# A decoder step on one core: quantising by masks on exponent bits, four scatters moved into the expert tiles, and a flag made on chip

## What is computed

```python
x = layernorm(x + tanh_attention(x))
x = layernorm(x + cross_attention(context, context, x, mask))
x = layernorm(x + quantised_linear(x))
x = layernorm(x + normed_attention(x))
x = layernorm(x + sparsemax_attention(x, context, context))
x = layernorm(x + mixture_of_experts(x))
```

```python
scales = max(max(abs(blocks), axis=-1) / 7.5, 1e-30)
q = nearest_on_grid(blocks / scales)      # 0, 0.125 ... 7.5; a tie goes to the lower value
out = (xq * xs) @ (wq * ws).T + bias
```

```python
topk_ids, topk_val = argmax(logits), max(logits)
xs = x * sigmoid(topk_val)
routed = (silu(xs @ gate[e]) * (xs @ up[e])) @ down[e]     # e = topk_ids of the row
out = shared + routed
```

## Time and profile before

| | us |
|---|---|
| median of the runs | 3414.75 |
| lowest and highest run | 3407.99, 3420.42 |
| the profiled execution, its own time | 3409.47 |
| its span in the trace | 3407.8 |
| quantised stage, 1245 to 1384 | 139 |
| sparsemax stage, 1795 to 2984 | 1189 |
| small stage of the flag, up to the first load of the expert stage | 2989 to 2994 |
| route block, 2994 to 3164 | 170 |
| expert tiles, 3164 to 3408 | 244 |

### The profile page before, as it was taken

One profiled execution on the slowest core, in us unless ns is written; L12 is line 12 of the kernel. 1 busy time (PEld: TensorE's weight loads), 2 busy tenths in 40 slices (PEclk: granted clock), 3 DMA queues, 4 the chain that ended last, 5 costly groups with the idle time before them and its releaser, 6 DMA issues. The chain is left out here.

```text
span 3407.8 us, 70871 instructions
## 1 busy us (share of the span) xinstructions
PE 2892.1 (85%) x23440; PEld 1868.3 (55%) x23440; DVE 2300.0 (67%) x10040; ACT 1990.0 (58%) x5876; POOL 1525.7 (45%) x2396
## 2 busy tenths in 40 slices
PE   8999997799999943599985888888888888779897
PEld 4555565476766732355552444454445444456897
DVE  2444545477777779467665999999999999622232
ACT  3333331477777730377763989898889988731111
POOL 0122212356666536566652444445454444405454
PEclk9999998799999976799986889888998988789999
DMA  2000000211111101100101000000000000063796
GB/s 75 14 23 15 18 13 17 61 46 44 47 44 47 43 27 46 42 27 27 31 23 44 17 23 20 23 18 19 23 20 23 20 23 16 5 234 145 266 350 221
DMA packets 106071, 190.86 MB, mean 56 GB/s; under 512 B 11891, under 2 KB 86906, under 8 KB 100446
## 3 DMA queue, kind: packets, MB, share of 16 engines
q1 hardware_dynamic: 101374, 176.34, 15.6%
q0 software_dynamic: 4320, 9.86, 0.8%
HBM read 145.22 MB, written 42.90 MB: 55 GB/s over the span
## 5 line engine op out<-in xcount | busy, mean ns | idle before, releaser
L3099 DVE MAX8 sa_cand<-sa_s 128x8 f32<-128x45 f32 (+3 forms) x3328 | 399.7, 190 | 31.2 <-ACT sa_s L2945 31.2
L914 ACT ACTIVATE ca_p<-ca_sm,ca_nb 100x361 f32<-100x361 f32 x512 | 301.0, 589 | 173.7 <-DVE ca_nb L995 173.3
L729 POOL TENSOR_SCALAR ca_p<-ca_p,ca_rec 100x361 f32<-100x361 f32 x512 | 282.2, 573 | 250.0 <-DVE ca_rec L1009 250.0
L2704 POOL TENSOR_SCALAR sa_s<-sa_s,sa_unit,sa_nu 128x361 f32<-128x361 f32 (+1 forms) x416 | 261.8, 651 | 204.0 <-DVE sa_nu L3191 204.0
L523 DVE RECIPROCAL ta_rec<-ta_den 128x400 f32<-128x400 f32 x64 | 169.6, 2650 | 246.4 <-PE ta_den L384 246.4
L2828 PE MATMUL sa_tr<-sa_ident,sa_s 128*128 128x128 f32 (+3 forms) x1248 | 230.1, 304 | 113.0 <-ACT sa_pT L2979 98.5
L995 DVE CUSTOM_DVE_ANT_0 ca_sm<-ca_sc,ca_mb 100x361 f32<-100x361 f32 x512 | 249.8, 526 | 59.5 <-PE ca_sc L816 59.4
L2961 ACT ACTIVATE sa_spare_a<-sa_s,sa_nu 128x361 bf16<-128x361 f32 (+1 forms) x416 | 247.3, 595 | 57.4 <-DVE sa_nu L3193 57.4
L2694 POOL TENSOR_TENSOR sa_over<-sa_cand,sa_tc 128x280 f32<-128x280 f32 (+3 forms) x128 | 99.6, 778 | 400.5 <-DVE sa_tc L3118 262.9
L288 POOL TENSOR_SCALAR_AFFINE_SELECT ta_pT<-ta_pT 100x400 f32<-100x400 f32 x128 | 66.6, 545 | 450.7 <-ACT ta_pT L466 450.7
L2828 PEld LDWEIGHTS sa_tr<-sa_ident,sa_s 128*128 128x128 f32 (+3 forms) x1248 | 164.8, 160 | 181.9 <-ACT sa_pT L2979 127.5
(11 more groups left out here) (314 smaller groups left out, 7195.1 us busy)
## 6 DMA issues: line engine op xcount, KB each, us to landing
me_we<-m_experts SPq DMA_DIRECT2D x40, 1024.0 KB, 7.1
me_wd<-m_experts SPq DMA_DIRECT2D x40, 512.0 KB
ca_cTs<-cT SPq DMA_DIRECT2D x32, 361.0 KB
sa_cTs<-cT SPq DMA_DIRECT2D x32, 361.0 KB
rows_acc<-me_zeros SPq DMA_DIRECT2D x1, 7196.0 KB
rows_in<-me_zeros SPq DMA_DIRECT2D x1, 7168.0 KB
ea_near<-rows_acc SPq DMA_DIRECT2D x40, 128.5 KB, 5.6
ea_xe<-rows_in SPq DMA_DIRECT2D x40, 128.0 KB
```

The costliest lines, as they stand in the source:

```text
L729: ins = pool.tensor_scalar(p[:, r, j, :], p[:, r, j, :], rec[:, r, j:j + 1], 1.0, ALU.mult, ALU.mult)
L914: act.activation(p[:, r, j, :], sm[:, r % 2, j, :], ACT.Exp, bias=nb[:, r % 2, j:j + 1], scale=-1.0, accum_out=den[:, r, j:j + 1]).then_in ...
L2704: pool.tensor_scalar(s[0:rows, u, i, :], s[0:rows, u, i, :], unit[0:rows, :], nu2[0:rows, i:i + 1], ALU.mult, ALU.add).then_inc(p_done.sem, 1)
L3099: ins = dve.max(cand[0:rows, i, q, :], s[0:rows, u, i, PART[q]:PART[q + 1]])
```

## The change

**In the quantised stage** the scale that divides is kept apart from half of it, which multiplies the result. The power of two of each number is now taken from its bits: one mask keeps the exponent (`pw`), another keeps and inverts it (`fl`), so that a product with the second brings the number near one; there it is rounded in one instruction by a constant, ties are put right in two, and one more multiplies by the power. The chain has 12 instructions.

**Between the sparsemax and the expert stage** PE transposes `top` into one row, and DVE makes the flag of it in the same block; the store of `sum_max`, the wait for it, and the stage `unfinished` are gone.

**In the expert stage** the couples 10 and 11 (tiles 20 to 23), the last in `DOWNS`, aren't scattered in the route block but by POOL at the start of `expert_tiles`. SP loads the rows of the first four tiles in the route block, once all scatters to `rows_in` have landed, and one identity serves both blocks.

```diff
-                chain.then(dve.tensor_scalar(scale_, amax[:, 0:nb], 1 / 7.5, 1e-30, ALU.mult, ALU.max))
-                chain.then(dve.reciprocal(inv[:, 0:nb], scale_))
+                chain.then(dve.tensor_scalar(amax[:, 0:nb], amax[:, 0:nb], 1 / 7.5, 1e-30, ALU.mult, ALU.max))
+                dve.tensor_scalar(scale_, amax[:, 0:nb], 0.5, None, ALU.mult)
+                chain.then(dve.reciprocal(inv[:, 0:nb], amax[:, 0:nb]))
...
-                chain.then(dve.tensor_tensor(near_, t, t, ALU.mult))
-                dve.tensor_scalar(tied, near_, 4.0, ONE, ALU.is_ge, ALU.mult)
-                chain.then(dve.tensor_scalar(magic, near_, 16.0, 2 * ONE, ALU.is_ge, ALU.mult))
-                chain.then(dve.scalar_tensor_tensor(magic, tied, ONE, magic, ALU.add, ALU.add))
-                chain.then(dve.tensor_tensor(near_, t, magic, ALU.add))
-                chain.then(dve.tensor_tensor(near_, near_, magic, ALU.subtract))
-                chain.then(dve.tensor_tensor(tied, near_, t, ALU.subtract))
-                chain.then(dve.scalar_tensor_tensor(tied, tied, 2 * PER, magic, ALU.mult, ALU.is_ge))
-                chain.then(dve.scalar_tensor_tensor(tied, tied, 1 / PER, magic, ALU.mult, ALU.mult))
-                dve.tensor_tensor(near_, near_, tied, ALU.subtract).then_inc(done, 1)
+                dve.tensor_scalar(bits(power), bits(t), EXPONENT, None, ALU.bitwise_and)
+                chain.then(dve.tensor_scalar(bits(flip), bits(t), EXPONENT, EXPONENT, ALU.bitwise_and, ALU.bitwise_xor))
+                chain.then(dve.scalar_tensor_tensor(t, flip, 2.0, t, ALU.min, ALU.mult))
+                chain.then(dve.tensor_scalar(near_, t, MAGIC, MAGIC, ALU.add, ALU.subtract))
+                chain.then(dve.scalar_tensor_tensor(t, near_, STEP / 2, t, ALU.subtract, ALU.is_equal))
+                chain.then(dve.scalar_tensor_tensor(near_, t, -STEP, near_, ALU.mult, ALU.add))
+                dve.scalar_tensor_tensor(near_, power, 1.0, near_, ALU.max, ALU.mult).then_inc(done, 1)
...
-            sp.wait_ge(top_step, 1)
-            sp.dma_start(sum_max, top[:, :]).then_inc(top_out, 16)
             for u in range(2):
                 sp.wait_ge(*stored[u].at(B // 2, 0))
-            sp.wait_ge(top_out, 16)
...
+            pe.wait_ge(top_step, 1)
+            pe.transpose(proj[0:1, 0:S], top[:, :], ident[0:S, 0:S]).then_inc(top_turned, 1)
...
+            dve.wait_ge(top_turned, 1)
+            dve.tensor_reduce(high[:, :], proj[0:1, 0:S], AX.X, ALU.max).then_inc(top_step, 1)
+            dve.wait_ge(top_step, 2)
+            dve.tensor_scalar(late[:, :], high[:, :], 1.0 + SUM_ERROR, None, ALU.is_gt).then_inc(top_step, 1)
+            dve.wait_ge(top_step, 3)
+            dve.tensor_copy(flag, late[:, :]).then_inc(top_step, 1)
+            dve.wait_ge(top_step, 4)
...
-            sp.wait_ge(early_in, 2 * DEEP * 16)
+            sp.wait_ge(rows_sent, 1)
+            rows_in_t = rows_in.rearrange("(t p) d -> t p d", p=P)
+            for n in range(DEEP):
+                sp.dma_start(xe[:, n, :], rows_in_t[n]).then_inc(early_in, 16)
+            sp.wait_ge(early_in, 3 * DEEP * 16)
...
+                    if n not in late_tiles():
+                        pool.indirect_dma_start(rows_acc, bass.IndirectOffsetOnAxis(ap=slot_i[:, n:n + 1], axis=0),
+                                                acc[:, n, :], None).then_inc(acc_sent, 16)
+                if d == COUPLES - 4:
+                    pool.wait_ge(sent, 16 * TILES)
+                    pool.sem_inc(rows_sent, 1)
...
+                if i or not loaded:
+                    sp.wait_ge(*etr_done.at(n, 1 - DEEP))
+                    sp.dma_start(xe[:, s, :], rows_in_t[first + n]).then_inc(xe_in[s].sem, 16)
...
-            identity(pool, ident, setup, 0)
             pool.memset(half[:, :], -0.5).then_inc(setup, 1)
-            pool.wait_ge(setup, 3)
+            if loaded:
+                for n in late_tiles():
+                    pool.indirect_dma_start(rows_acc, bass.IndirectOffsetOnAxis(ap=slot_i[:, n:n + 1], axis=0),
+                                            acc[:, n, :], None).then_inc(acc_sent, 16)
+            pool.wait_ge(setup, 1)
```

More of the change, by code:

```diff
@@ L1071, in quantised_linear @@
     NB = X_COLS // BLOCK
-    ONE = 1.5 * 2.0 ** 20
-    PER = 1.5 * 2.0 ** 23
-    STEPS = 13
+    EXPONENT = 0x7F800000
+    STEP = 0.25
+    MAGIC = STEP * 1.5 * 2.0 ** 23
+    STEPS = 10
     with ExitStack() as ctx:
@@ L2428, in _, with packed_sparse_attention @@
             dve.tensor_reduce(top[:, :], worst[:, :], AX.X, ALU.max).then_inc(top_step, 1)
-def packed_sparse_attention(nc, x, cT, heads4, Wq, bq, Wk, bk, Wv, bv, WoS, bo, out, sum_max):
+def packed_sparse_attention(nc, x, cT, heads4, Wq, bq, Wk, bk, Wv, bv, WoS, bo, out, flag):
     H, HD = 16, 16
@@ L2497, in packed_sparse_attention @@
         top = a.sb("top", [S, 1])
+        high = a.sb("high", [1, 1])
+        late = a.sb("late", [1, 1])
         pT = a.sb("pT", [P, NK, H * S])
@@ L3738, in _, with late_tiles, expert_tiles @@
                 add_shared(d)
-def expert_tiles(nc, tag, experts, rows_in, rows_acc, out, owner_i, first, count, we, wd, loaded, acc_sent):
+def late_tiles():
+    couples = (TILES + 1) // 2
+    last = couples - 3
+    return [n for c in range(last, couples - 1) for n in range(2 * c, 2 * c + 2)]
+def expert_tiles(nc, tag, experts, rows_in, rows_acc, acc, slot_i, out, owner_i, first, count, we, wd, xe, ident, loaded, acc_sent):
     with ExitStack() as ctx:
         a = Place(nc, ctx, tag)
-        ident = a.sb("ident", [P, P])
-        xe = a.sb("xe", [P, DEEP, D])
         xeT = a.sb("xeT", [P, 2, D])
@@ L3839, in _ @@
             open_all(pe, etr_done, g_done, up_done, y_done)
-            pe.wait_ge(setup, 2)
             def turn_rows(n):
                 s = n % DEEP
-                pe.wait_ge(*xe_in[s].at(n // DEEP, 1))
+                pe.wait_ge(*xe_in[s].at(n // DEEP, 0 if loaded else 1))
                 pe.wait_ge(*eT_done.at(n, -1))
@@ L3948 @@
 SUM_ERROR = 2.0 ** -17
-def unfinished(nc, sum_max, flag):
-    with ExitStack() as ctx:
-        a = Place(nc, ctx, "uf")
-        row = a.sb("row", [1, S])
-        high = a.sb("high", [1, 1])
-        late = a.sb("late", [1, 1])
-        row_in = a.sem("row_in")
-        step = a.sem("step")
-        block = ctx.enter_context(nc.Block())
-        @block.sync
-        def _(sp):
-            sp.dma_start(row[:, :], sum_max.rearrange("s o -> o s")).then_inc(row_in, 16)
-        @block.vector
-        def _(dve):
-            dve.wait_ge(row_in, 16)
-            dve.tensor_reduce(high[:, :], row[:, :], AX.X, ALU.max).then_inc(step, 1)
-            dve.wait_ge(step, 1)
-            dve.tensor_scalar(late[:, :], high[:, :], 1.0 + SUM_ERROR, None, ALU.is_gt).then_inc(step, 1)
-            dve.wait_ge(step, 2)
-            dve.tensor_copy(flag, late[:, :]).then_inc(step, 1)
-            dve.wait_ge(step, 3)
 def build(nc, t):
@@ L3986, in build @@
     normed_attention(nc, rows[2], t["parity01"], t["causal"], t["a1_WkqT"], t["a1_WvT"], t["a1_WuT"], t["a1_ln"], rows[3])
-    sums = [dram(f"sum_max{n}", (S, 1)) for n in range(2)]
+    sum_max = dram("sum_max", (S, 1))
     sparse = lambda newton, tag, sum_max: sparse_attention(
@@ L3990, in build @@
         t["c1_Wo"], t["c1_bo"], rows[4], sum_max, newton, tag)
-    packed_sparse_attention(nc, rows[3], t["cT"], t["heads4"], t["c1_Wq"], t["c1_bq"], t["c1_Wk"], t["c1_bk"], t["c1_Wv"],
-                            t["c1_bv"], t["c1_WoS"], t["c1_bo"], rows[4], sums[0])
     with nc.sbuf_tensor("late", [1, 1], I32) as flag:
-        unfinished(nc, sums[0], flag[:, :])
+        packed_sparse_attention(nc, rows[3], t["cT"], t["heads4"], t["c1_Wq"], t["c1_bq"], t["c1_Wk"], t["c1_bk"], t["c1_Wv"],
+                                t["c1_bv"], t["c1_WoS"], t["c1_bo"], rows[4], flag[:, :])
         late = nc.values_load(flag[0:1, 0:1], min_val=0, max_val=1)
         with nc.If(late == 1):
-            sparse(ALL_STEPS, "sb", sums[1])
+            sparse(ALL_STEPS, "sb", sum_max)
         mixture_of_experts(nc, rows[4], t["m_gate"], t["m_shared"], t["m_experts"], t["m_consts"],
```

26 lines of the change are left out of this document (12 added, 14 removed).

## The result

The changed kernel takes 3380.13 us in the median (3378.05 to 3382.45), the one before beside it 3414.15: 34.0 us less, a ratio of 0.990 with a 95% interval of 0.988 to 0.991. The prediction was 3375, with a range from 3361 to 3389.

What follows compares the result with a forecast made beforehand. It took three limits: a DVE instruction chain, a hand-over in which nothing computes, and a wait for a tiny transfer. −27.3 − 8.3 − 4.1 = −39.7 us from the 3414.75 median gave 3375, range 3361 to 3389.

Steps and rivals of the forecast that it cites:

- Part 1: Quantised stage: a shorter DVE chain gives −28.1 us, less 0.8 for a late load: −27.3, ends −24 and −28.
- The price of the masks on int32: Quantised stage: each int32 mask over 1280 columns takes 0.82 us; at 1.49, 8.0 us less gain, chance 0.08.
- the load: Quantised stage: SP's load of the group three ahead, behind the normed rows' store, lands 0.4 us late, twice.
- The rival that had the old 2 us: Quantised stage: the load stays 2 us late in two groups; part 1 −24.1, total −36.5, 3378 us; chance 0.17.
- fast masks that hold the port like the others: Quantised stage: fast DVE masks also lock out POOL, so the load is 1.3 us late, twice; part 1 is −25.5.
- Part 2: End of sparsemax stage: no wait for the sums (−5.14) and a shorter hand-over (−3.15): −8.3 us, ends −6.5 and −9.
- the small stage: Between sparsemax and expert stages: without the block reading the sums back, 5.35 us to the first load becomes 2.20: −3.15.
- The slower rival: Sparsemax flag: a sum passed through PE exceeds its bound, the full stage reruns, at least 1189 us: 4564; chance 0.015.
- Part 3: Route block into expert tiles: −2.5 us for scatters and −1.65 for early tiles and identity: −4.1, ends −3.5 and −7.5.
- The reading of the price as one by the number of scatters: Route block's end: 3.40 us extra after 50 scatters is POOL's price for scattering; by number, 46 take 0.27 less.
- (b): Block ends: four fewer scatters save 0.27 us in the route block, the next block's end costs as much more: nothing.
- Their cover: Expert tiles' start: four moved scatters, 5 us on POOL, are hidden; SP is let through 6 to 9 us after PE's start.

Runs made afterwards that it cites:

- part 2 alone: The kernel before with only the sparsemax flag made on chip, no store of sums or small stage: 3406.60 us, 0.998 of the kernel before.
- the kernel that moves the norms away: The changed kernel with the fourth group's load ahead of the first store and the quantised norms on ScalarE instead of POOL: 3370.70 us against 3375.40.
- the store put back: The changed kernel with SP again storing the 100 sums in 100 pieces and waiting for them, read by nothing: 3382.82 us in one run.
- The two stores: The changed kernel plus an unread store of the 100 sums, as 100 pieces of 4 bytes or one of 400: 3382.82 and 3371.93 us.
- the run that puts them back: The changed kernel with all 25 scatters of sums in the route block again, early loads and shared identity kept: 3385.27 us in one run.
- the run with 21 fewer: The changed kernel with all 25 scatters of sums at the expert tiles' start, 25 scatters in the route block instead of 46: 3399.90 us, one run.
- part 1 alone: The kernel before with only the quantised stage's masks on exponent bits: 3387.39 us against 3414.58, ratio 0.993.
- part 3 alone: The kernel before with only four late scatters, early loads of rows and one identity: 3411.29 us, ratio 0.9985.
- the second result: The changed kernel run again with nothing edited, beside the kernel before: 3375.40 against 3417.26 us, ratio 0.988.

## Why the prediction held, and where it was off

**Part 1**, −27.3 forecast, −25.0 measured. The arithmetic held: the weights went from 9.28 to 6.91 us between the first reductions (−2.37, −2.35 forecast), the undisturbed first group from 17.38 to 12.24 (−5.14, −5.15 forecast), two of the three periods fell by 5.3. The price of the masks on int32, the largest open one, was the lower end, 0.82. The step that was off is the load: I put it 0.4 us late in two groups, from norms that pass at each boundary of DVE's chain and end 15.5 to 17.3 us after L1330. They ended after 17.6, as if the fewer instructions changed little, the data were there 5.4 us behind that where I had put 5.1, and the load was 1.88 us late in the first of the two. The rival that had the old 2 us was nearer for this group; in the second the wait was nil, since POOL ran alone while DVE waited in the first, and had caught up (its norms ended 16.3 us after L1330). In sum the load cost 2.0 us in place of 0.8.

Then 1.1 us were lost behind the masks, which I had called untouched: from the last L1330 of a full group to the next stage's first load 23.2 us in place of 22.1. There PE's first transpose came 0.3 later, behind POOL, and one pair of products took 1.79 in place of 1.03 us. The granted clock of PE (the number behind the instructions) from 3.4 to 5.3 us after that transpose, before, with the change, and in the kernel with part 2 alone, whose masks are the old ones:

```profile
1369.09:1370.99 1.90, 1.90 (x12) 1.00 0.00 0
```

```profile
1345.83:1347.73 1.90, 1.90 (x8) 0.58 0.00 0
```

```profile
1372.49:1374.39 1.90, 1.90 (x7) 0.50 0.00 0
```

With the old masks, too, the clock has risen late, and that trace lost 1.3 us behind them (23.4 us, its stage 141.8 in place of 140.2). So most of the 1.1 us is PE's clock, and not a price that only the new masks pay; whether they make a late rise likelier is open (23.1 to 23.8 us in all eight traces that have them and POOL's norms, 22.0, 22.1 and 23.4 in the three with the old ones).

That POOL and DVE hold each other up was argued in the prediction and is shown by the kernel that moves the norms away. There the Trainium skill's rule ("SBUF — State Buffer", the two separate sides) agrees with the trace, also on the point on which it differed from my middle value, fast masks that hold the port like the others: beside the norms the rounding took 1.07 in place of 0.83. It stood at −25.5, with 2.6 us for the load, against 2.0 measured. That its total lies so close to −25.0 is in part luck, since the 1.1 us behind the masks are no part of it.

**Part 2**, −8.3 forecast, −8.0 measured, by the steps as put: 1.5 us of wait for the rows, the flag covered by the norm (ready 1.2 us before POOL's norm is done), and a hand-over behind that wait of 2.5 us (2966.72 + 0.29 + 1.5 = 2968.5, to 2971.04), which had been put at 2.2. That is the 0.3 that is missing. Of the 8.0 us the store put back takes 4.5, so the small stage was worth the other 3.5 (5.1 and 3.15 forecast). The two stores show that the first of these terms was the price of one transfer's form, which the prediction had taken from the row without a reason. The slower rival didn't come: the flag stayed down, and the expert stage follows in every trace.

**Part 3**, −4.1 forecast, −4.1 measured for the gap (6.1 us forecast, 6.15 measured), and each of its steps: −2.5 for the scatters (2.56 by the run that puts them back), −1.65 for loads and identity (1.55). The reading of the price as one by the number of scatters, which the prediction drew from one subtraction of two hand-overs, is borne out by the run with 21 fewer and by the DRAIN rows; the subtraction gave 68 ns each, the rows 82. Moving four scatters from a block to the next saves nothing of it, as said under (b): 0.33 us less at the one end, 0.33 more at the other. Their cover held: SP came to the sums after 8.0 us, inside the 6 to 9 estimated, and DVE never waited for them. What I had not put in, 0.8 us from a first product at a higher clock (2.97 for 3.75), came and went between runs: the same program had 3.76 in its second trace.

**The sum** by stages is −37.6 against −39.7, and nearly all of the difference is the load and the tail of part 1. The medians gave −34.0 and −41.9. What made the first smaller is, as far as the traces show it, no step of the prediction: PE's clock in stages that the change doesn't touch. (The mean granted clock was 0.909 to 0.912 in the four runs of the first comparison, 0.912 to 0.914 in those of the second.) The stretch of 30 us from some 10 us after the normed attention's start shows where it begins, in the two traces of the same changed kernel, the slower first:

```profile
1372.70:1402.70 30.00, 23.26 (x99) 11.36 (x100) 7.92 (x46) 13.72 (x41) 16.96 (x6) 0.56 0.05 12
```

```profile
1375.70:1405.70 30.00, 22.38 (x130) 10.79 (x130) 9.36 (x55) 15.08 (x46) 16.97 (x6) 0.73 0.06 18
```

The clock was granted at 0.56 in the one and at 0.73 in the other (0.5 is the lower level, 1.2 GHz, 1.0 the higher, 2.4 GHz), behind the same hand-over in which PE idled; 99 against 130 PE instructions got done. Over twelve traces here, whose code is the same in that stage, it took 405.5 to 417.6 us: 409.3 with part 1 alone, 409.9 with part 3 alone, 417.6 in one run and 407.6 in another with all of part 1. Why the clock rises early in one execution and late in the next isn't settled by these runs. Long and short ones come from the same program, so it is no price that the change pays each time. That the change makes a long one likelier isn't excluded: the three traces above 411 us are among the nine with part 1, and the three without it lie between 408.6 and 409.9. The 34.0 us were well inside the stated range all the same; that the second result, 3375.40, meets the 3375 to a microsecond is luck, since the sum of the stages is 2 us short of the forecast.

## What to carry to other kernels

Cost a chain by counting its instructions at the rates in the trace, then look for the engine that shares its data: when the chain becomes shorter, the neighbour's pace and what the two cost each other set the new period, and it pays to move that work as well (here to an idle engine, with an earlier load, for some 6 us more). At a block's end look at what the issuing engine has to finish and not only at what the data need: number of scatters, size and number of the pieces of a store. And when a small gain is to be judged, add up the stages that the change touches; one stage of the rest differed by 10 us between two runs of the same program.

## What the runs showed of the hardware

At the end of a block in which POOL has issued indirect scatters, its DRAIN took 82 ns for each (2.10 us after 25, 3.33 after 40, 3.65 after 44, 3.82 after 46, 5.37 after 65), also for those issued tens of microseconds before. A store of 100 numbers of 4 bytes from 100 partitions held its waiter for 5.7 to 6.3 us, the same bytes from one partition for no longer than a store of 100 KB beside it, in 100 pieces of 1 KB (1.2 us). Bitwise masks on int32 ran on DVE as fast as comparisons and products with constants on float32: 0.82 us for 1280 columns. And PE's granted clock at the start of the same stage lay between 0.56 and 0.73 in executions of the same program.
